# Self attention run continuously, an earlier addition in the cross attention, and a recurrence step whose gates are transposed together

## The reference, cut to what matters

```
# layer 1 (the change touches its two attentions), H = 16 heads of 64
h1 = adaln(x);  x = softmax(q k^T / 8) v @ wo + bo + x      # q, k, v from h1 (self attention)
h2 = adaln(x);  x = the same with k, v from the context     # cross attention
h3 = adaln(x);  x = glu_ff(h3) + x
# layer 2: causal attention and a mixture of 8 experts
# layer 3 (the change touches its end), 512 steps in order, h starts as the conditioning vector
proj = h @ W;  attn = softmax(enc . proj);  context = attn . enc
gx = [x_t, context] @ kernel + bias;  gh = h @ recurrent_kernel
z = sigmoid(xz + hz);  r = sigmoid(xr + hr);  cand = tanh(xh + r * hh)
h = z * h + (1 - z) * cand
# layer 4: experts that choose tokens
```

## Time and profile before

| | us |
|---|---|
| median of 3 executions | 2896.53 |
| lowest and highest | 2892.72, 2897.61 |
| profiled execution, its own time | 2893.86 |
| its span | 2892.1 |
| self attention, about | 50 to 596 |
| cross attention and feed forward, about | 596 to 740 |
| recurrence with background, about | 980 to 2777 |

### The profile page before, as it was taken

The page is one execution under the profiler, slowest core; times in us unless marked ns, Lnnn a source line. Parts: engine busy times, 40 slices in busy tenths (PEclk is TensorE's granted clock), DMA queues, the critical chain, the costliest instruction groups (busy, mean ns, idle before and its releaser), DMA issues. The chain is left out here.

```text
span 2892.1 us, 137366 instructions
## 1 busy us (share of the span) xinstructions
PE 2466.8 (85%) x57363; PEld 1671.7 (58%) x57364; DVE 1903.3 (66%) x7219; ACT 1577.2 (55%) x5266; POOL 994.6 (34%) x1992
## 2 busy tenths in 40 slices
PE   7999999977898799889899898898879877666669
PEld 4666666666455455566565565666656545444449
DVE  4666666776452577777677677777767765776553
ACT  4666666643363366666666576666657533333322
POOL 2000000033020167555777465566636411111126
PEclk9999999999898899999999999999999999999989
DMA  4000000000001100001100011000001000000013
GB/s 151 5 5 5 5 5 5 5 12 1 7 23 55 54 14 18 15 21 45 31 17 14 11 36 38 23 13 14 7 7 36 13 20 6 7 7 7 6 47 87
DMA packets 51896, 64.76 MB, mean 22 GB/s; under 512 B 7432, under 2 KB 36560, under 8 KB 51152
## 3 DMA queue, kind: packets, MB, share of 16 engines
q1 hardware_dynamic: 47184, 50.32, 5.8%
q0 software_dynamic: 4096, 5.67, 1.0%
HBM read 46.38 MB, written 9.60 MB: 19 GB/s over the span
## 5 line engine op out<-in xcount | busy, mean ns | idle before, releaser
L2268 POOL TENSOR_TENSOR gru_terms<-gru_states,gru_signs 128x8 f32<-128x8 f32 x512 | 103.7, 203 | 794.0 <-DVE gru_states L2553 689.4
L2009 PE MATMUL gru_ps_sr<-score_w,gru_states 128*32 128x78 f32 x4096 | 175.7, 243 | 183.5 <-DVE gru_states L2553 173.8
L2188 ACT ACTIVATE gru_p_t<-gru_ps_tc,gru_negmax 128x12 f32<-128x12 f32 x512 | 138.9, 271 | 338.3 <-DVE gru_negmax L2522 322.1
L2191 ACT ACTIVATE gru_th_r<-gru_pre_r 128x32 f32<-128x32 f32 x512 | 119.2, 233 | 303.4 <-DVE gru_pre_r L2535 303.2
L2244 POOL TENSOR_SCALAR bg_probs<-bg_probs,bg_arsum 128x256 f32<-128x256 f32 (+2 forms) x192 | 240.7, 1254 | 84.5 <-DVE gru_c_in L2542 78.5
L1759 PE MATMUL gru_ps_tc<-ctx_gate_w,gru_p_t 128*4 128x64 f32 x12288 | 267.8, 220 | 0.2
L371 ACT ACTIVATE self_probs<-self_sc,self_negmax 128x512 f32<-128x512 f32 x256 | 174.3, 684 | 167.4 <-DVE self_negmax L428 167.4
L1759 PE MATMUL gru_ps_sr<-ctx_gate_w,gru_p_t 128*4 128x34 f32 x12288 | 189.7, 195 | 76.1 <-ACT gru_p_t L2188 73.5
L2009 PEld LDWEIGHTS gru_ps_sr<-score_w,gru_states 128*32 128x32 f32 x4096 | 81.2, 107 | 293.0 <-DVE gru_states L2553 274.9
L1759 PEld LDWEIGHTS gru_ps_sr<-ctx_gate_w,gru_p_t 128*4 128x4 f32 x12288 | 120.4, 86 | 195.0 <-ACT gru_p_t L2188 179.0
L2021 PE MATMUL gru_ps_ox<-late,gru_states 128*4 128x128 f32 x4096 | 226.3, 273 | 0.0
(11 more groups left out here) (420 smaller groups left out, 6567.5 us busy)
## 6 DMA issues: line engine op xcount, KB each, us to landing
bg_w<-in_moe_w SPq DMA_DIRECT2D x48, 256.0 KB, 3.0
bg_wa<-in_wqkv SPq DMA_DIRECT2D x24, 192.0 KB, 2.4
moe_w<-in_moe_w SPq DMA_DIRECT2D x16, 256.0 KB, 3.6
best_w_sb<-in_ec_w SPq DMA_DIRECT2D x16, 256.0 KB, 3.0
x_products<-late SPq DMA_DIRECT2D x16, 240.0 KB, 2.4
late<-x_products SPq DMA_DIRECT2D x240, 16.0 KB
cross_scratch<-ctab_raw SPq DMA_DIRECT2D x16, 154.0 KB
cross_outs<-cross_scratch POOLq DMA_DIRECT2D x4, 576.0 KB, 6.0
```

The costliest lines, as they stand in the source:

```text
L2009: last = pe.matmul(ps_s[32 * b:32 * b + 32, :], state(t)[:, b:b + 1].broadcast_to([P, 32]), score_w[:, b, 0:CTX + 1], start=True, stop=Tru ...
L2188: act.activation(p_t[:], ps_t, ACT.Exp, bias=negmax[:, 0:1]).then_inc(s_exp, 1)
L2191: act.activation(th_r[:, 1:64:2], pre_r[:], ACT.Tanh, scale=0.5).then_inc(s_thr, 1)
```

## The change

Self attention: the function serves this one layer alone now; `turn_probs(3)`, `values(2)`, `values(3)` and `project_out` of a unit are done inside the next unit, v has two buffers and shares a bank with the projected output, and the orders of ScalarE and VectorE are made to fit. The product of v moves to the end of the unit before. Cross attention: `add_out` comes at the start of the round with u % 8 = 6 in place of the end of the one with 7. Recurrence: r, candidate and z are put side by side in rows and transposed by one instruction of 96 columns, the old state's part by another of 32; the scan of the candidate's input, both tanh and the factors then work on columns, 8 or 4 wide, and the tanh writes the state's terms directly. The factors move from ScalarE to VectorE. Waits are reordered accordingly.

```diff
@@ self attention: TensorE
+            project_qk(0)
+            project_v(0)
+            for it in range(N):
+                scores(it, 0)
+                if it:
+                    turn_probs(it - 1, 3)
+                    values(it - 1, 2)
+                scores(it, 1)
+                turn_probs(it, 0)
+                if it:
+                    values(it - 1, 3)
+                scores(it, 2)
+                turn_probs(it, 1)
+                if it:
+                    project_out(it - 1)
+                values(it, 0)
+                scores(it, 3)
+                turn_probs(it, 2)
+                if it + 1 < N:
+                    project_qk(it + 1)
+                values(it, 1)
+                if it + 1 < N:
+                    project_v(it + 1)
+            turn_probs(N - 1, 3)
+            values(N - 1, 2)
+            values(N - 1, 3)
@@ SP
                 sp.wait_ge(s_pv, pair * B)
+                sp.wait_ge(s_pk, pair * B)
@@ ScalarE
+                exponentials(it, 0)
+                if it:
+                    take_turned(it - 1, 3)
+                exponentials(it, 1)
+                take_turned(it, 0)
+                exponentials(it, 2)
+                take_turned(it, 1)
+                exponentials(it, 3)
+                take_turned(it, 2)
+                if it + 1 < N:
+                    take_qk(it + 1)
+                    take_v(it + 1)
@@ VectorE
+                maxima(it, 0)
+                normalise(it, 0)
+                maxima(it, 1)
+                normalise(it, 1)
+                if it:
+                    take_out(it - 1)
+                maxima(it, 2)
+                normalise(it, 2)
+                if it:
+                    add_out(it - 1)
...
+                maxima(it, 3)
+                normalise(it, 3)
@@ cross attention: VectorE
             for u in range(2 * NTT + 2):
+                if u % (2 * NT) == 6 and 2 * NT < u < 2 * NTT:
+                    add_out(u // (2 * NT) - 1)
...
-                if u % (2 * NT) == 7 and u > 2 * NT:
-                    add_out(u // (2 * NT) - 1)
@@ recurrence: tiles
+        own = sb("own", P)
+        pre_r, gate_rows, gate_cols, c_in = sb("pre_r", 32), sb("gate_rows", 96), sb("gate_cols", 192), sb("c_in", 2 * B)
+        th_r, c_and_z = gate_rows[:, 0:32], gate_rows[:, 32:96]
+        gates_turned, own_turned = gate_cols[:, 1:192:2], gate_cols[:, 64:128:2]
+        r_cols, c_cols, z_cols = gate_cols[:, 0:2 * B], gate_cols[:, 64:64 + 2 * B], gate_cols[:, 129:129 + 2 * B:2]
@@ recurrence: ScalarE
-                act.activation(th_r[:, 1:64:2], pre_r[:], ACT.Tanh, scale=0.5).then_inc(s_thr, 1)
-                act.wait_ge(s_precz, t + 1)
-                act.activation(th_z[:], pre_z, ACT.Tanh, scale=0.5).then_inc(s_thz, 1)
+                act.activation(th_r, pre_r[:], ACT.Tanh, scale=0.5).then_inc(s_thr, 1)
+                act.wait_ge(s_gcols, t + 1)
+                act.activation(th_z[:], z_cols, ACT.Tanh, scale=0.5).then_inc(s_thz, 1)
                 act.wait_ge(s_cin, t + 1)
-                act.activation(cand[:], c_in[:, 1:64:2], ACT.Tanh).then_inc(s_cand, 1)
-                act.wait_ge(s_tz, t + 1)
-                act.activation(factors[:, 2:3 * B:3], th_z_t[:, 0:B], ACT.Copy, bias=0.5, scale=-0.5).then_inc(s_onez, 1)
+                act.activation(terms[:, 0:3 * B:3], c_in[:, 1:2 * B:2], ACT.Tanh).then_inc(s_cand, 1)
@@ recurrence: VectorE, behind c_and_z
-                dve.wait_ge(s_thr, t + 1)
-                dve.wait_ge(s_precz, t + 1)
-                dve.tensor_tensor_scan(c_in[:], th_r[:], own[:, 192:256], 0.0, ALU.mult, ALU.add).then_inc(s_cin, 1)
-                dve.wait_ge(s_thz, t + 1)
                 dve.wait_ge(s_olds, t + 1)
                 if t:
                     dve.wait_ge(s_hist, t)
-                dve.transpose(th_z_t[:], th_z[:]).then_inc(s_tz, 1)
+                dve.transpose(own_turned, own[:, 96:P]).then_inc(s_hcols, 1)
+                dve.wait_ge(s_thr, t + 1)
+                dve.wait_ge(s_precz, t + 1)
+                dve.transpose(gates_turned, gate_rows[:]).then_inc(s_gcols, 1)
+                dve.wait_ge(s_gcols, t + 1)
+                dve.wait_ge(s_hcols, t + 1)
+                dve.tensor_tensor_scan(c_in[:], r_cols, c_cols, 0.0, ALU.mult, ALU.add).then_inc(s_cin, 1)
+                dve.wait_ge(s_thz, t + 1)
+                dve.tensor_scalar(factors[:, 2:3 * B:3], th_z[:], -0.5, 0.5, ALU.mult, ALU.add).then_inc(s_onez, 1)
                 dve.wait_ge(s_cand, t + 1)
-                dve.transpose(terms[:, 0:96:3], cand[:]).then_inc(s_tc, 1)
-                dve.wait_ge(s_tc, t + 1)
                 dve.wait_ge(s_onez, t + 1)
```

344 lines of the change are left out of this document (99 added, 245 removed).

## The result

The changed kernel takes 2878.92 us (median of 4 runs, 2875.82 to 2881.91); the kernel before took 2894.62 in the same session. The ratio is 0.9945, with a 95% interval of 0.9928 to 0.9962: 15.7 us less, where I had forecast 54. The profiled execution has a span of 2877.9 for 2892.1, and I place the 14.2 between them by stage. All lengths are between the first or last instructions of a stage; a step of the recurrence runs from one start of the state's scan to the next.

What follows compares the result with a forecast made beforehand. Bounds: TensorE in self attention, TensorE waiting for VectorE's addition in cross attention, a latency chain of 512 steps in the recurrence. Gains 23 + 18 + 13 = 54 us; 2896.5 - 54 = 2842, own range 2828 to 2857, range asked for 2810 to 2872.

Steps and rivals of the forecast that it cites:

- Self attention, 23 us: Self attention: two TensorE idle times go, units shrink from 16.66 to 15.9 us, 0.75 x 31 = 23 us gained.
- blocks that stood in twos are parted: Self attention: separating paired scores and paired values costs TensorE 0.20 us each, 0.40 per unit.
- Rival 3: Self attention keeps its pace, a loop over ScalarE replacing the idle times: 23 us less gain, 2865; chance 0.10.
- Cross attention, 18 us: Cross attention: the earlier addition to y removes 12.6 us of TensorE waiting and 5 us of lower clock.
- 0.11 less: Recurrence: wide transpose to state's scan takes 0.74 us, where the old stretch took 0.85.
- the other branch: Recurrence: tanh of z, then VectorE's factors' tensor_scalar, ends at 0.69 plus 0.04 us, a tie with the 0.74 chain.
- The 380 others x 0.70: Recurrence: steps not held by GpSimd, 0.70 of them (358 of 512) gaining 0.105 us each: -28 us.
- 132 steps held: Recurrence: GpSimd's scaling holds the state's scan, 132 x 0.70 steps longer by 0.16 us: +15 us.
- the first (the scan slips in ahead of GpSimd): Recurrence: the state's scan beats GpSimd's scaling, so all 512 steps gain, 43 us for 13: 2812; chance 0.13.
- The second (wide transpose over 0.3): Recurrence: the 96-column transpose pays for stepped output, 0.34 us, chain 0.82, recurrence +14 us: 2870; chance 0.12.
- The fourth: Recurrence: GpSimd locks out VectorE's new tensor_scalar, about 1.1 us in each of 132 steps: slower, 2943; chance 0.05.

Runs made afterwards that it cites:

- Run 5: The changed kernel with the self attention's product of v put directly behind those of q and k, ahead of values(1): 2875.03 us, ratio 0.9923.
- run 4: The changed kernel with the tanh of z, the factors' tensor_scalar and one of the two waits left out: 2865.86 us, ratio 0.9890.
- run 3: The changed kernel with GpSimd's scaling released sooner, by the softmax's exponential (s_exp) in place of the scan of the candidate's input: 2868.78 us.

## Why the prediction was wrong

The direction was right, the size was not, and the time lies above my range. By the steps of the prediction:

- **Self attention, 23 us: 14.6 alone, 16.2 in the trace.** Both idle times went, as I had them. The mis-sized term is "blocks that stood in twos are parted", taken as 0.40: it is 16.12 - (16.66 - 1.12) = 0.58. The unit has 13 changes of kind for 9 before. The two parted pairs are two of the four, and these I had counted; the other two I had not, and one of them is the product of v, put between values and scores. Run 5 shows it: v moved back beside q and k gives 0.19. The Trainium skill ("TensorEngine Tiling (Array Packing)", section "Key Properties") says that a change of tiling mode drains the engine. The trace agrees in that a change costs time, with 1.02 for 0.92 where the next block has another tile; a drain by itself isn't seen in it. Rival 3 did not come: the q and k copies are in time.
- **Cross attention, 18 us: 14.8 alone.** The 12.6 of waiting went in full. Clock and shorter busy time gave 3.8 (145.7 to 141.9) for my 5, and 2.0 came back as a longer wait for ScalarE. I had taken the first from the clock alone and the second not at all.
- **Recurrence, the chain, "0.11 less": 0.02.** The wide transpose took 0.279 for my 0.26, the scan 0.174 for 0.17, the tanh 0.208 for 0.20, and with three hand-overs of 0.03 this chain would be 0.762 for my 0.74, as run 4 (no z) shows. The step that failed is "the other branch", which I had at "0.69 plus 0.04, a tie". It ended at 0.721, and the scan, which waits for it last of two, came 0.103 behind it: 0.824. I had taken one price for every hand-over, and the second of two waits costs 0.10. That is the 0.062 between the two runs.
- **"The 380 others x 0.70": -28 forecast.** Even with the right size a mean over all steps would have misled. With z left out the chain, from the start of the tanh of r to that of the scan, was 35.6 us shorter in all, of which 14.3 reached the recurrence's end; the last 112 steps kept 7.8 of 8.2, while the first two attentions kept 2.1 of 9.4 (2.9 of it went into scans held longer). A count of steps in which the weight load waits for the state (358 of 512) says that it waits, not that it waits long or that nothing behind it will be late; how far TensorE's background work sets each step was not measured.
- **"132 steps held", +15: the price was right.** 0.51, 0.61 and 0.72 behind GpSimd's start by width, as taken from the earlier trace rows; GpSimd came at 0.66 for my 0.63. The three attentions got 1.9 + 1.8 + 10.9 = 14.6 us longer. That this meets the +15 is partly luck: these phases have 229 steps and not 132, and among them steps that I had expected to gain. The place was wrong, too: of 28 us of scan time 13.6 fall into the first two attentions, where most of them don't reach the end.
- Together: phases with held steps +14.6 for +15, all others +2.5 for -28. That these others lost time was not expected at all. For the third experts' phase it is clear of the spread (275.7 to 277.2 in three traces with the new step, 274.3 to 274.7 in three with the old one); for the second it is not (158.0 to 159.3 for 157.2 to 158.6). With z left out the third is at 272.3. What makes the new step slower there was not tried.

The rivals: the first (the scan slips in ahead of GpSimd) failed by 0.12 us, as the scan came at 0.16 behind GpSimd for the 0.04 that it needs. The second (wide transpose over 0.3) was wrong in its cause, so that its 2870 was the nearest is luck. The page that I had set beside it (the Trainium skill, "Vector Engine (DVE) Microarchitecture Reference", section 5.2) has rows for outputs that hop much further, and they don't carry over to this transpose: 32, 64 and 96 columns with a step of 2 took 0.203, 0.246 and 0.279, so 1.2 ns for a column. At the page's 1.7 to 2.5 the widest would be 0.31 to 0.36, an estimate from the 0.203 of 32 columns. The fourth did not occur in the changed kernel, where the tensor_scalar took 0.17 throughout; run 3 shows that its mechanism exists, once GpSimd starts sooner.

## What to carry to other kernels

Price a shortened chain phase by phase, from the phases in which it is the bound, and check each release of another engine against it: an instruction that comes 0.1 us later or earlier can fall into a lock that it missed before. Where an instruction of the chain waits for two others, don't call a near tie free: here the wait named last cost 0.10 and the one named first 0.03, so name the later one first, and see whether one of the two can be done without. To learn which of them sets the start, look at the steps in which one side happens to be late. When idle time on TensorE is filled by interleaving, count how often neighbouring blocks change their tile shape, in the new order as a whole and not only for the blocks that are moved.

## What the runs showed of the hardware

- **GpSimd's hold on VectorE has two stretches.** A tensor_scalar on GpSimd with 256, 384 or 512 columns (0.93, 1.25, 1.58 us) holds VectorE's scan with both inputs in SBUF until 0.508, 0.613 or 0.720 after its start; a scan that begins within 0.04 gets through at its 0.18, in some 50 steps after the change. Behind that stretch instructions pass again, but a tensor_scalar that begins 0.82 behind a 384-wide scaling, or 0.60 to 0.75 behind a 256-wide one, is held until 0.02 behind GpSimd's end. VectorE's c_and_z, with an input in PSUM, was not longer beside it (0.28). The Trainium skill ("SBUF — State Buffer", section "Who interferes with whom") lets the first have the shared ports for its whole instruction, and names two inputs in SBUF and tensor_scalar as cases. The trace agrees with the cases (the tensor_scalar took up to 0.49 us for 0.17) and not with the length.
- **The second of two waits on VectorE is dear.** Where the state's scan waits for two semaphores, it begins 0.032 behind the instruction whose semaphore it waits for first, or 0.101 to 0.103 behind the one that it waits for last, whichever is later. It makes no difference which engine the signal comes from (VectorE's tensor_scalar 0.103, ScalarE's tanh 0.101), or that the other wait has long been met (0.21 us earlier in the run without the tensor_scalar). With one wait alone it is 0.032. Why is not shown.
- **TensorE pays for changes between tiles,** 0.08 to 0.21 us each in the self attention by the kinds that meet, with no idle time in the trace: the price is inside the busy time.
